# Two sparse graph-attention layers on one core: six of x's eight load blocks moved from SyncE's queue to ScalarE's

## What is computed

```python
h = jnp.maximum(_layernorm(x, axis=-1), 0.0)
# layer 0: cosine scores, softmax over the neighbours
Qn, Kn = _cos_normalize(h @ Wq.T), _cos_normalize(h @ Wk.T)
att = softmax(where(adj > 0, Kn @ Qn.T, NEG))
x = x + 0.5 * (mask * (att @ h) + (1 - mask) * h) + 0.5 * h
h = jnp.maximum(_layernorm(x, axis=-1), 0.0)
# layer 1: additive scores from two vectors, softmax over the neighbours
g = h @ W.T + b_W
e = leaky_relu((g @ a1)[:, None] + (g @ a2)[None, :] + b_a, 0.2)
x = x + softmax(where(adj > 0, e, NEG)) @ g
```

## Time and profile before

| what | us |
|---|---|
| median of 3 runs | 1671.44 |
| lowest, highest | 1669.94, 1672.61 |
| the profiled execution, its own time | 1664.98 |
| its span, first to last instruction | 1663.2 |
| busy in the span: PE, DVE, ACT, POOL | 1140.0, 1041.8, 891.0, 1120.6 |

### The profile page before, as it was taken

The page is one execution under the profiler, slowest core; times in us unless marked ns, Lnnn a source line. Parts: engine busy times, 40 slices in busy tenths (PEclk is TensorE's granted clock), DMA queues, the critical chain, the costliest instruction groups (busy, mean ns, idle before and its releaser), DMA issues.

```text
span 1663.2 us, 22697 instructions
## 1 busy us (share of the span) xinstructions
PE 1140.0 (69%) x6317; PEld 898.4 (54%) x6317; DVE 1041.8 (63%) x4012; ACT 891.0 (54%) x2786; POOL 1120.6 (67%) x1170
## 2 busy tenths in 40 slices
PE   5877677777676677676556647666666767666765
PEld 3544344444444454454546537666666766666655
DVE  5976688888788887888763314444444444444444
ACT  3543455556556556556768735555555555555433
POOL 1224777777777767766777157777777777777775
PEclk9998788988989988889766657787878787878878
DMA  9999999999999999999222022222222222222222
GB/s 353 420 372 365 405 408 405 406 407 406 405 402 388 399 399 396 397 394 375 64 55 59 22 47 60 58 60 60 60 60 60 60 60 61 59 60 60 61 60 49
DMA packets 108396, 361.69 MB, mean 217 GB/s; under 512 B 24421, under 2 KB 57576, under 8 KB 75496
## 3 DMA queue, kind: packets, MB, share of 16 engines
q1 hardware_dynamic: 55272, 277.05, 41.4%
q0 software_dynamic: 35840, 74.62, 17.5%
q10 hardware_dynamic: 17152, 8.52, 1.9%
HBM read 347.38 MB, written 12.72 MB: 217 GB/s over the span
## 4 chain that ended last, share of the span: by engine, by line
POOL 35%; issue 12%; PE 2%; ACT 1%; DMA 0%; DVE 0%; POOLq 0%; ACTq 0%; DVEq 0%
POOL arena L559 18%; POOL arena L554 13%; POOL arena L968 4%; PE ps L1043 1%; PE ps L517 1%; ACT prod L1134 0%; DMA arena<-tab,idx_all 0%; PE ps L377 0%; ACT diag L1145 0%; PE ps L599 0%; DMA tab<-tw 0%; ACT arena L506 0%; ACT arena L508 0%; ACT arena L504 0%; ACT h L355 0%
## 5 line engine op out<-in xcount | busy, mean ns | idle before, releaser
L968 POOL DMA_INDIRECT arena<-tab,idx_all x576 | 564.0, 979 | 207.1 <-issue 167.7
L1012 PE MATMUL ps<-arena,fold 128*128 128x512 fp8e4 x1024 | 302.0, 427 | 194.4 <-DMA arena<-in_adj_dram 193.8
L559 POOL DMA_INDIRECT arena<-tab,idx_all x320 | 303.3, 948 | 97.5 <-issue 97.5
L554 POOL DMA_INDIRECT arena<-tab,idx_all x224 | 214.4, 957 | 111.7 <-issue 68.0
L1012 PEld LDWEIGHTS ps<-arena,fold 128*128 128x128 bf16 x1024 | 89.3, 102 | 360.2 <-DMA arena<-in_adj_dram 267.7
L1134 ACT ACTIVATE prod<-prod,arena 128x128 f32<-128x128 f32 x576 | 221.9, 388 | 34.3 <-DVE prod L1349 34.3
L686 DVE SCALAR_TENSOR_TENSOR arena<-ps,s_all,arena 128x512 f32<-128x512 f32 (+1 forms) x112 | 66.9, 633 | 252.0 <-PE ps L575 252.0
L575 PE MATMUL ps<-ident,arena 128*128 128x128 f32 x704 | 133.3, 358 | 77.6 <-DMA arena<-tab,idx_all 77.5
L517 PE MATMUL ps<-arena 128*128 128x26 f32 x704 | 103.9, 297 | 105.4 <-ACT keys L526 93.4
L629 ACT ACTIVATE arena<-arena,negm 128x517 f32<-128x517 f32 (+1 forms) x64 | 56.8, 887 | 216.4 <-DVE negm L696 216.4
L575 PEld LDWEIGHTS ps<-ident,arena 128*128 128x128 f32 x704 | 118.5, 258 | 82.7 <-DMA arena<-tab,idx_all 82.7
(11 more groups left out here) (200 smaller groups left out, 2205.2 us busy)
## 6 DMA issues: line engine op xcount, KB each, us to landing
arena<-in_adj_dram SPq DMA_DIRECT2D x256, 1024.0 KB
arena<-tab,idx_all POOLq DMA_INDIRECT x1120, 2.6
tab<-arena ACTq DMA_DIRECT2D x16, 260.0 KB, 14.5
tab<-tw ACTq DMA_DIRECT2D x32, 130.0 KB, 10.3
res<-in_x_dram SPq DMA_DIRECT2D x8, 512.0 KB, 6.6
out_dram<-arena SPq DMA_DIRECT2D x64, 64.0 KB, 1.6
prod<-in_L_gnn_Wq_dram SPq DMA_DIRECT2D x1, 64.0 KB
prod<-in_L_gnn_Wk_dram SPq DMA_DIRECT2D x1, 64.0 KB
```

The source lines that it names most:

```text
L554: pool.indirect_dma_start(out=GS[h % 2][:, c, :], out_offset=None, in_=tab1, in_offset=bass.IndirectOffsetOnAxis(ap=idx_all[:, at, slot:sl ...
L559: pool.indirect_dma_start(out=GO[q][:, s, :], out_offset=None, in_=tab1, in_offset=bass.IndirectOffsetOnAxis(ap=idx_all[:, t, s:s + 1], ax ...
L968: pool.indirect_dma_start(out=G[q][:, s, :], out_offset=None, in_=tab0, in_offset=bass.IndirectOffsetOnAxis(ap=idx_all[:, t, s:s + 1], axi ...
L1012: last = nc.tensor.matmul(keys_ps[t % 2], fold[:, PIECE_BITS * f + b, :], ring8[m % RING][:, b * WORDS:(b + 1) * WORDS], start=False, stop ...
```

## The change

Blocks 0 and 1 of x stay first on SyncE's queue, now both ahead of the weights. The six pieces of the adjacency come after the weights. Blocks 2 to 7 of x are issued by ScalarE, right behind the load of its activation table and ahead of `deviations(0)`.

```diff
+        def load_x(eng, b):
+            eng.dma_start(res[:, 8 * b:8 * b + 8, :], x_t[:, 8 * b:8 * b + 8, :]).then_inc(s_x[b], 16)
+
         def loads_sync(sp):
-            def load_x(b):
-                sp.dma_start(res[:, 8 * b:8 * b + 8, :], x_t[:, 8 * b:8 * b + 8, :]).then_inc(s_x[b], 16)
-
-            load_x(0)
+            load_x(sp, 0)
+            load_x(sp, 1)
             for k, m in enumerate((wq, wk, w)):
                 sp.dma_start(wraw[:, k * D:(k + 1) * D], m).then_inc(s_w, 16)
...
-            for b in range(1, 4):
-                load_x(b)
             for m in range(RING):
                 load_piece(sp, m)
-            for b in range(4, 8):
-                load_x(b)
             sp.wait_ge(s_edged, 1)
...
                 act.preload_act_table_set("sqrt_and_others")
+                for b in range(2, 8):
+                    load_x(act, b)
                 for b in range(4):
                     deviations(b)
                 relu(0)
```

## The result

The changed kernel took 1680.51 us (median of 5 runs, 1677.81 to 1682.59), the kernel before 1671.44 us (5 runs beside it, 1668.89 to 1672.61). The ratio is 1.0061, 95% interval 1.0046 to 1.0075: slower by 9.1 us as the medians stand, and by 7.7 to 12.5 us by the interval. The changed kernel's profiled execution took 1680.51 us, with a span of 1678.6.

A forecast was written before the change was run, and what follows sets the result against it. The stream of adjacency pieces, bound by DMA bytes, was taken to have no slack before 160 us. Terms of -1.5 + 13.7 = +12.2 us gave 1677.2 us on the profiled execution and 1683.6 us on the median; range 1670 to 1691 us.

The forecast's parts named there:

- ScalarE is held: At the start, ScalarE's six x issues block until about 2,400 packets are left, so ScalarE is free at 27.1 us.
- lower bound of 1678 us: Low end of the likeliest case: ScalarE may leave some 1,000 packets more outstanding, 4 or 5 us less.
- Packet for packet: With both queues full, the DMA engines move equal packet counts from each, 54 a us, whatever the packet size.
- rival of turns by bytes: DMA queues take turns by bytes: ScalarE free at 13.3 us, 1.5 us gained, 1669.9 us; chance 0.05.
- SyncE held along with ScalarE: Rival at the start: a held ScalarE holds SyncE too, delaying weights and pieces; 0.9 us lost, 1672.3 us; chance 0.09.
- What follows: After ScalarE's late start, the first fold comes at 42.4 us and piece 6 moves at 44.4 us, 12.2 us late.
- Nothing takes it up again: The adjacency stream behind piece 6 keeps its 12.2 us delay, which reaches the end of the kernel.
- Covered weights: At the start, weights land at about 11 us behind x's block 1; that 3 us delay is covered by ScalarE's lateness.
- Edge rows, and x behind the pieces: On SyncE's queue, edge rows land earlier and four x blocks go from behind the pieces; worth nothing by itself.
- The first rival's two halves: ScalarE isn't held: 1.5 us gained (1669.9 us), or x's backlog ahead of stores turns it into 5 us lost; chance 0.17.

## Why the prediction was right

*ScalarE is held.* Right. Free at 26.5 us where I had 27.1. The packet records give the allowance at the end of the third to sixth issue as 2,793, 2,752, 2,042 and 2,637 packets where I had 2,400 from one pair of SyncE's rows. Over all runs a held issue of x on ScalarE's queue ends with 2,029 to 2,793 left, and SyncE's issue of 12.17 us in the kernel before, which I didn't use for this, ends with 2,143 (2,048 of x, 95 of pieces).

That the two times agree to 0.6 us is partly luck. At 10.9 us ScalarE's queue had moved 2,647 packets, not 2,818, which is 3.2 us late at 54 a us; the allowance was 237 larger, which is 4.4 us early. The hold is steady only on one side: with 2,400 left it would have ended at 27.3 us, since the pieces run out there and the rest drains fast, but with 2,793 left at 23.6 us. My lower bound of 1678 us doesn't follow from my own rates. I had put 1,000 more packets of allowance at 4 or 5 us; the queue had moved those 2,744 at 12.0 us, and with ScalarE free at about that time (the kernel whose pieces wait for x) piece 6 is 1 us behind before and piece 44 ahead.

*Packet for packet.* Right. In the changed kernel, from 11 to 27 us:

```profile
q1 hardware_dynamic: 868, 6.15, 91.0%
q10 hardware_dynamic: 976, 0.49, 10.2%
```

Close to even, although one queue's packets are sixteen times the other's; from 12 to 26 us, with both queues full throughout, it is 757 and 758. The rival of turns by bytes falls with it. Equal totals alone don't say how many rows a turn takes, since nine of each in turn would give them too. But in every 0.3 us from 12 to 26 us the records have 11 to 16 rows of pieces and 12 to 24 of x, where one DMA engine needs 9 x 0.309 = 2.8 us for nine rows of a piece. That speaks for turns of one row, and against the Trainium skill's figure of 9 to 17 descriptors to a turn (DMA: Bandwidth & Descriptors, Queues, rings and completion order), if a row is one descriptor.

*SyncE held along with ScalarE.* It wasn't. While ScalarE's fourth issue (4.61 to 7.53 us) and fifth (7.56 to 18.24 us) stood, SyncE issued its six pieces:

```profile
6.58 2.80 SPq L210 DMA_DIRECT2D arena<-in_adj_dram  x6
```

0.47 us each. By the Trainium skill's account of an exclusively locked generator (Perfetto Trace Analysis, DMA Instruction — HWDGE (DVE, Sync)) I would have expected waits as long as ScalarE's. The longest of SyncE's other issues, a weight during ScalarE's third, was 1.63 us (0.57 us before), so locking for a moment isn't excluded; locking for the length of a hold is.

*What follows.* The first fold at 41.4 us where I had 42.4, piece 6 at 43.5 where I had 44.4: 11.5 us behind before, by the term 12.2.

*Nothing takes it up again.* Right in the first comparison, and only there is it shown: +11.5 at piece 6, +12.3 at piece 44, +13.6 at the first gather, +15.2 at the last. The profiled executions end 15.5 us apart, the medians 9.1 us, and the interval of 7.7 to 12.5 us takes in my 12.2. I predicted 1683.6 us and measured 1680.5; between these figures neither the marks nor the interval can tell an error of mine from the scatter of the stream, so that difference stays open. I added 6.5 us for the distance of before's profiled execution from its median; the changed kernel's profiled execution is its median, so those 6.5 us are all of the difference between 15.5 and 9.1.

*Covered weights.* They landed at 12.9 us, not 11; covered by the hold, save for the 0.8 us that stay open above. *Edge rows, and x behind the pieces:* the first fold's `extract` waited 1.29 us for TensorE instead of for the edge rows, and nothing came of it, as I had it.

*The first rival's two halves.* With the issues spread out the start gained 2.6 us at piece 6, and the backlog ahead of the stores left the first gather 8.1 us behind before; I had put the loss at up to 5 us.

## What to carry to other kernels

Before moving loads to the queue of an engine that computes, count their packets against what the queue takes before an issue is held (here 2,000 to 2,800 of 512 bytes, and some 1,700 with stores behind), and see what the other queues move meanwhile: beside 8 KB packets, 512-byte ones drained at 54 a us here instead of 668. Near that limit 54 packets are a microsecond, so leave room. An engine that is idle for nearly half of the kernel (ScalarE was busy for 891 of 1663 us) can still be first on the path at its start. Keep small-packet loads off a queue on which something later has to get through, and let large-packet streams wait for them if they are short.

## What the runs showed that I had not expected

Holding the large stream of the changed kernel back by 7 us brought it forward by 13 at piece 44. A queue's store issues are held by a backlog of loads as well: 5.42 and 8.91 us on an issue that otherwise takes 0.37 us. And one kernel can wait for different things in different sets of executions: the same folds waited 138 us for pieces in the first comparison and at most 8 in the experiments, so there a microsecond lost by the stream at the start need not show in the whole time.
